# Two neighbour sweeps of a graph kernel: five of 16 units unsplit in place of six, and one of eleven remainders made by VectorE

## What is computed

```python
h = jnp.maximum(_layernorm(x, axis=-1), 0.0)
x = x + jnp.matmul(adj.T, h) * inv_deg[:, None]     # inv_deg = 1 / adj.sum(axis=0), 0 where infinite
h = jnp.maximum(_layernorm(x, axis=-1), 0.0)
x1 = swish(adj @ h @ W + b)
x2 = swish(adj @ x1 @ W + b)
return x + x2
```

## Time and profile before

| | us |
|---|---|
| median of 3 runs | 687.6 |
| lowest and highest run | 684.11, 690.33 |
| the profiled execution, its own time | 688.42 |
| its span, first to last instruction | 686.6 |
| mean granted TensorE clock | 0.971 of full speed |

### The profile page before, as it was taken

How to read it: one execution, slowest core, us unless ns; L and a number is a source line. 1 busy time by engine, 2 the same in 40 slices (tenths; PEclk the granted TensorE clock), 3 DMA queues, 4 the chain that set the end, 5 groups by cost and what they waited for, 6 DMA issues and landing times.

```text
span 686.6 us, 6755 instructions
## 1 busy us (share of the span) xinstructions
PE 634.4 (92%) x2212; PEld 404.0 (59%) x2212; DVE 523.1 (76%) x516; ACT 301.4 (44%) x378; POOL 571.2 (83%) x287
## 2 busy tenths in 40 slices
PE   4888978999998988899999999999999999799994
PEld 2355545666665645556666666667666557466553
DVE  3965789979978839777787777878778778577871
ACT  1943243264272343646445445445444434245250
POOL 2288488689788857998999999999999789599693
PEclk9989999999999998999999999999999999899998
DMA  8999996989999899999999999919999999999941
GB/s 277 352 303 306 298 366 246 329 300 333 329 292 309 286 233 250 345 345 317 328 345 330 329 345 317 279 25 195 327 345 345 315 328 332 305 252 347 311 94 31
DMA packets 155762, 199.80 MB, mean 291 GB/s; under 512 B 5456, under 2 KB 138832, under 8 KB 155728
## 3 DMA queue, kind: packets, MB, share of 16 engines
q1 hardware_dynamic: 86672, 133.18, 62.5%
q10 hardware_dynamic: 69056, 66.20, 35.0%
HBM read 197.26 MB, written 2.10 MB: 290 GB/s over the span
## 4 chain that ended last, share of the span: by engine, by line
PE 55%; POOL 20%; issue 12%; DMA 4%; ACT 3%; DVE 3%; ACTq 1%; SPq 1%; POOLq 0%
PE dg L351 20%; POOL a_lo L701 11%; PE dg L368 9%; PE dg L357 9%; PE dg L358 9%; POOL at_lo L715 7%; PE m_ps L277 4%; DMA raw<-in_adj_dram 2%; PE m_ps L376 2%; DMA h<-in_x_dram 2%; POOL norm L684 1%; PE m_ps L295 1%; PE m_ps L282 1%; PE m_ps L283 1%; ACTq L217 1%
## 5 line engine op out<-in xcount | busy, mean ns | idle before, releaser
L715 POOL TENSOR_TENSOR at_lo<-turned,at_hi 128x1024 fp32r<-128x1024 f32 x160 | 379.8, 2414 | 33.1 <-ACT at_hi L455 28.3
L602 DVE STREAM_TRANSPOSE turned<-raw 128x1024 f32<-128x1024 f32 x256 | 304.1, 1224 | 95.7 <-PE dg L351 41.9
L455 ACT ACTIVATE at_hi<-turned 128x1024 fp32r<-128x1024 f32 x160 | 167.3, 1057 | 208.8 <-DVE turned L602 122.2
L701 POOL TENSOR_TENSOR a_lo<-raw,a_hi 128x1024 fp32r<-128x1024 f32 x66 | 155.1, 2387 | 46.7 <-ACT a_hi L425 44.7
L351 PE MATMUL dg<-turned,f_w 128*128 128x512 f32 x384 | 182.4, 597 | 1.3 <-issue 1.3
L559 DVE TENSOR_TENSOR dg<-raw,dg 128x2048 f32<-128x2048 f32 x60 | 137.5, 2291 | 35.5 <-DMA raw<-in_adj_dram 33.6
L357 PE MATMUL dg<-at_hi,f_hi 128*128 128x512 f32 x320 | 134.9, 422 | 11.5 <-ACT at_hi L455 11.5
L368 PE MATMUL dg<-at_lo,f_hi 128*128 128x512 f32 x320 | 130.9, 490 | 3.1 <-POOL at_lo L715 3.1
L358 PE MATMUL dg<-at_hi,f_lo 128*128 128x512 f32 x320 | 128.4, 401 | 0.0
L277 PE MATMUL m_ps<-raw,h 128*128 128x512 f32 x248 | 116.6, 617 | 11.1 <-DMA raw<-in_adj_dram 11.1
L351 PEld LDWEIGHTS dg<-turned,f_w 128*128 128x128 f32 x384 | 73.2, 191 | 57.0 <-issue 48.5
(11 more groups left out here) (47 smaller groups left out, 258.8 us busy)
## 6 DMA issues: line engine op xcount, KB each, us to landing
raw<-in_adj_dram SPq DMA_DIRECT2D x64, 1024.0 KB, 8.9
raw<-in_adj_dram ACTq DMA_DIRECT2D x122, 512.0 KB, 13.5
raw<-in_adj_dram SPq DMA_DIRECT2D x118, 512.0 KB, 11.7
x<-in_x_dram SPq DMA_DIRECT2D x16, 128.0 KB, 13.5
out_dram<-zs ACTq DMA_DIRECT2D x16, 128.0 KB, 10.9
h<-in_x_dram SPq DMA_DIRECT2D x1, 768.0 KB, 9.3
h<-in_x_dram SPq DMA_DIRECT2D x1, 256.0 KB, 3.3
w<-in_L_gnn_W_dram ACTq DMA_DIRECT2D x1, 64.0 KB, 3.0
```

The costliest lines, as they stand in the source:

```text
L455: act.activation(at_hi[:, s % RING3], turned[:, unit % TURN], ACT.Copy).then_inc(hi3_done, 1)
L602: dve.transpose(dst, src).then_inc(t3_done, 1)
L701: pool.tensor_tensor(a_lo[:, s % RING1], raw1[:, v % RAW1, i], a_hi[:, s % RING1].bitcast(f32), ALU.subtract).then_inc(lo1_done, 1)
L715: pool.tensor_tensor(at_lo[:, s % RING3], turned[:, unit % TURN], at_hi[:, s % RING3].bitcast(f32), ALU.subtract).then_inc(lo3_done, 1)
```

## The change

`WHOLE3` has five units in place of six: 0, 3, 7, 11 and 15. The other eleven of each group are split. Of these, unit 9 (`DVE_LO3`) has its remainder made by VectorE, right behind the transpose of the unit after it; GpSimd makes the other ten. The two engines count their remainders on semaphores of their own, and `wait_lo3` picks the one that a waiting engine needs. The ring sizes stay as they are; two buffers get smaller (`u`, and `gap`, which only fills room) so that the larger f2 and f3 tensors fit.

```diff
-WHOLE3 = (0, 3, 6, 9, 12, 15)
+WHOLE3 = (0, 3, 7, 11, 15)
+DVE_LO3 = (9,)
...
-        u = sb("u", [P, QT, P], into=sweep1)
+        u = sb("u", [P, QT - UC, P], into=sweep1)
...
-        gap = sb("gap", [P, 3 * 1024], into=sweep2)
+        gap = sb("gap", [P, 2560], into=sweep2)
...
-        hi3_done, lo3_done = sem("hi3_done"), sem("lo3_done")
+        hi3_done = sem("hi3_done")
+        lo3_pool, lo3_dve = sem("lo3_pool"), sem("lo3_dve")
...
+        def by_dve(unit):
+            return PIECES[unit // QU][1] * QU + unit % QU in DVE_LO3
+
+        def wait_lo3(eng, unit):
+
+            mine = [s for s in splits3 if by_dve(s) == by_dve(unit)]
+            eng.wait_ge(lo3_dve if by_dve(unit) else lo3_pool, mine.index(unit) + 1)
+
+        def lo3(eng, unit):
+            s = split3(unit)
+            eng.wait_ge(hi3_done, s + 1)
+            if s >= RING3:
+                eng.wait_ge(rest3_done, s - RING3 + 1)
+            return eng.tensor_tensor(at_lo[:, s % RING3], turned[:, unit % TURN], at_hi[:, s % RING3].bitcast(f32),
+                                     ALU.subtract)
...
-                    eng.wait_ge(lo3_done, split3(back) + 1)
+                    wait_lo3(eng, back)
...
-                pe.wait_ge(lo3_done, split3(unit) + 1)
+                wait_lo3(pe, unit)
...
-                    act.wait_ge(lo3_done, s - RING3 + 1)
+                    wait_lo3(act, splits3[s - RING3])
...
                 turn3(unit)
+                if by_dve(unit - 1):
+                    lo3(dve, unit - 1).then_inc(lo3_dve, 1)
...
-                if not whole3(unit):
-                    lo3(unit)
+                if not whole3(unit) and not by_dve(unit):
+                    lo3(pool, unit).then_inc(lo3_pool, 1)
```

More of the change, by code:

```diff
@@ L708, in lo_h2 @@
                                    f2_hi[:, tiles].bitcast(f32), ALU.subtract).then_inc(h2_ready, 1)
[L710 to L716, removed]
             def lo_x1(r):
```

## The result

The changed kernel took 720.0 us (median of 6 runs, 719.1 to 728.2) against 688.2 us for the kernel before (684.1 to 692.8): ratio 1.049, 95% interval 1.045 to 1.054. It is 32 us slower, where 9 us were forecast and 706 us was the end of the range. The profiled execution took 719.7 us with a span of 717.8, 31.2 us more than the span of before.

The account below looks back on a forecast made before the run. The prediction took PE to bound the middle, with GpSimd 1 to 3% behind and becoming the new bound. Start +2.8, middle +2.1 and late +4.6 made +9.5 us, 697 for a median; range 683 to 706, the forecast's own 692 to 702.

Parts of the forecast that it names:

- The prices of PE: In the sweeps: 1.72 us per whole unit, 1.395 per split unit, so a pair of groups becomes 49.7 us.
- The +2.8 us for the start: Start, 249 to 304 us: two collisions at 1.03 us plus 0.7 us for one more f2_lo on GpSimd.
- its sum would be PE's gain alone: Claim that, without the Trainium skill's contention rule, the forecast would hold only PE's 5.2 us gain.
- its 1.03 us: GpSimd's loss taken for each of 16 collisions with VectorE's subtraction: longest remainder 3.425 less median 2.394 us.
- The turned ring of five: Around unit 9: GpSimd works 4.7 us on units 6 and 8 against DVE's 1.22 + up to 3.15; no further loss.
- the middle, forecast at +2.1 us: Middle, 304 to 511.9 us: GpSimd busy 210.0 us with eight collisions and one f_lo, against the present 207.9.
- the late part, at +4.6: Late, 511.9 to 676 us: GpSimd's 149.0 us plus 19.7 idle for ScalarE make 168.7, against 164.1.
- rival 3: VectorE's line: waits for at_hi and GpSimd's port delay transposes, GpSimd idles; +10 on the forecast, 707 us; chance 0.13.
- the whole bound: Most that late transposes behind the subtraction could cost if late each time: 16 x 1.3 = 20 us.
- at_hi of unit 9 ... should be there: Before the subtraction: at_hi's 1.06 us copy is about as long as unit 10's 1.22 us transpose, so no wait.
- Rival 1: TensorE stays the bound, the collision hidden in GpSimd's slack or cheap: 5.2 us gained, 682.4 us; chance 0.20.
- Rival 2: Late part's 19.7 us of idleness absorbs its share; only start and middle pay: +4.7, or 692 us; chance 0.13.

Follow-up runs that it names:

- e2_psum: Changed kernel with VectorE's subtraction in the same place with the same waits, second input an idle PSUM region in place of at_hi: 701.8 us, ratio 1.016.
- e11_turn_psum: Changed kernel, whole, with unit 9 turned into an idle PSUM region in place of the SBUF ring: 702.3 us, ratio 1.018.
- e1_none: Changed kernel without VectorE's remainder of unit 9; whoever waited for it waits for at_hi of unit 9: 690.3 us, ratio 1.002.
- e12_turn_psum_late: Changed kernel with unit 9 turned into idle PSUM and the subtraction behind the transpose of unit 12: 685.6 us, ratio 0.996.
- e7_add_psum: Kernel before plus one VectorE subtraction in each of groups 2 to 15, second input in idle PSUM, no wait: 687.5 us, ratio 0.999.
- e6_add_sbuf: Kernel before plus one VectorE subtraction with two SBUF inputs in each of groups 2 to 15, no wait: 700.4 us, ratio 1.014.
- e5_wait_only: Changed kernel where VectorE waits in the same place but subtracts nothing; others wait for at_hi of unit 9: 691.3 us, ratio 1.004.
- e14_both: Changed kernel with unit 9 turned into PSUM, subtraction behind unit 12's transpose, and the residual add fed from PSUM: 691.3 us, ratio 1.004.
- e3_two_later: Changed kernel with VectorE's subtraction one transpose later, behind that of unit 11: 710.4 and 711.3 us, two more runs 722.9 and 724.0.
- e9_sbuf_no_wait: Changed kernel without unit 9's remainder; VectorE instead subtracts two SBUF regions without a wait in groups 2 to 15: 711.6 us, ratio 1.030.

## Why the prediction was wrong

Step by step, from the kernel before to the changed one (medians): 688; with the new spacing and no subtraction 690; with the wait 691; with 1.22 us of work behind the wait 702; with both inputs in SBUF 720.

By stages, from the starts of the copies that end groups 1, 9 and 15 (us, one profile each; e2_psum's is of its fastest run, e11_turn_psum's of its slowest):

| kernel | start to group 1 | group 1 to 9 | group 9 to 15 |
|---|---|---|---|
| before | 310.9 | 201.1 | 163.9 |
| e1_none | 314.0 | 199.2 | 162.8 |
| e12_turn_psum_late | 314.2 | 198.9 | 162.9 |
| e2_psum | 311.9 | 204.0 | 167.4 |
| e11_turn_psum | 314.7 | 203.9 | 173.9 |
| changed | 314.8 | 217.9 | 174.4 |
| e7_add_psum | 309.4 | 201.1 | 161.7 |
| e6_add_sbuf | 308.9 | 218.2 | 161.0 |

In the middle the second SBUF input makes 14 us and the place 5. In the late part it makes nothing in e6_add_sbuf, and 0.5 to 7 us between the changed kernel and the two with PSUM; the rest there goes with the place.

**Right.** The prices of PE: a pair of groups takes 49.7 us when nothing else holds it (e1_none). The collision: VectorE's remainder is 1.23 us of work plus waiting, GpSimd's takes up to 3.4 us, and a group in which VectorE gets in at the end of the running remainder takes the forecast 24.5 us (24.60). The +2.8 us for the start fit the 3.2 measured by luck: e1_none has the same 3.2 without any subtraction. The Trainium skill's rule, weighed in the prediction, bears out as far as two SBUF inputs being what matters ("SBUF — State Buffer", "Who interferes with whom"): e7_add_psum against e6_add_sbuf, 13 us. How long the second one waits is not settled by "waits in full", as the prediction has it: in e6_add_sbuf two whole remainders that started later ran first, and the measurement decides. The prediction's sentence that without the rule its sum would be PE's gain alone is wrong too: its 1.03 us come from its own rows.

**The step that failed** is this one: "The turned ring of five lets GpSimd work on units 6 and 8 meanwhile (4.7 us) against 1.22 + up to 3.15 on DVE. I count no further loss". It counted on an overlap that isn't there: the middle, forecast at +2.1 us, took 17 more, and the late part, at +4.6, took 10. Two things in it were off.

First, 3.15 us isn't the most that a subtraction takes. In the residual adds of the earlier trace rows VectorE waited for the one remainder that was running, and I took that as the rule. In the changed kernel three took about 5 us, as a further remainder went ahead, and in e6_add_sbuf the longest 6.9, as two did. With 1.49 us of waiting and 5.36 of subtraction, VectorE's line stood still for 6.85 us in the group shown, against the 4.7 us of work that GpSimd was to have. Three collisions in the profile of before said too little about the longest wait.

Second, GpSimd's next at_hi comes from a transpose behind the waiting subtraction. The longer GpSimd holds VectorE up, the more surely it runs dry itself. That is rival 3, VectorE blocks the line, which had a chance of 0.13 and half of its bound. Its mechanism is the measured one: GpSimd's idle time for at_hi grew by 23 us (51.4 against 28.3), where the forecast had none and the whole bound was 20. GpSimd's loss in its own instructions, the only loss that the forecast counted for the collision, was 8.4 us on the remainders where 16 x 1.03 = 16.5 was taken, since in the dear cases GpSimd had run out of work by the time VectorE ran, and where silu comes first some fell on the f_lo splits.

**"at_hi of unit 9 ... should be there"** failed too: VectorE stood 23.8 us for it, 12 times. The prediction weighed only the copy's 1.06 us and left out that ScalarE issues loads ahead of it (2.61 us in the group shown). The silu and x1 copies, which come ahead of it in four groups, it gave to rival 3 with some 2.7 us of waiting; in three of these groups VectorE stood 2.8 to 3.5 us. By itself the wait costs about 1 us (e5_wait_only), with 1.22 us of work behind it 11 (e2_psum), and nothing with the subtraction two transposes further back (e12_turn_psum_late).

**Rival 1** (PE stays the bound, 5.2 us gained) is what happens in the middle of e1_none and e12_turn_psum_late. Even there the gain is not all kept: the start is 3 us longer.

**Rival 2** has no support: the late part grew by 10 us, and GpSimd's idle time in it from 21.3 to 27.1 us.

What stays open: what decides whether VectorE gets in after one remainder or after two or three. In e6_add_sbuf an instruction issued 1.25 us after the start of GpSimd's took 2.2 us in some cases and 6.9 in others. It wasn't tried further. Also open are the longer start, how the late part's loss divides between place and collision, and e14_both.

## What to carry to other kernels

An instruction on VectorE with both inputs in SBUF, beside a GpSimd that reads SBUF back to back, is to be priced by what stands behind it on VectorE's queue: if GpSimd's own next input comes from there, the two starve each other. Feed one of its inputs from PSUM where room is free (here 702 us in place of 720), and put it so far back that its wait is over when its turn comes (686 in place of 702). Even so the kernel was only as fast as before: PE's gain of 2 us in the middle went into a start that was 3 us longer. A duration from a profile that has three collisions is a lower bound of the worst, not the worst.

## What the runs showed of the hardware

A VectorE instruction with two SBUF inputs doesn't always get its turn at the end of GpSimd's running instruction: in e6_add_sbuf a 1.23 us instruction took 6.9 us, through the rest of one and two whole GpSimd instructions of 2.4 us, and it ran when GpSimd was idle. In the 14 cases of 4.5 us and more (three each in the changed kernel, e3_two_later and e9_sbuf_no_wait, five in e6_add_sbuf) it was so each time. The transpose from SBUF to PSUM and the subtraction with one input in PSUM showed no such wait (e11_turn_psum: means of 1.231 and 1.224 us over 16, beside the same GpSimd work).
